# Half swap of a rotary embedding on ScalarE, its sine part and sum, four product steps and the lists of steps of a three-layer block changed

## The chip, the cores and the metric

One core of one Trainium2 chip. The metric is the device time of one launch in microseconds (us), the median of several runs. A core has TensorE (PE, matmuls; PEld is its weight load), VectorE (DVE), ScalarE (ACT), GpSimd (POOL) and SyncE (SP, which issues the DMAs here). Every engine works through its own list of instructions in order and meets the others only at semaphores.

## The reference, cut to what matters

The input x is 8 sequences ("batches") of 512 tokens with 128 features. Three layers follow one another:

```python
# 1. delta net, 8 heads x 16, two decays j per head
q, k = elu(x@Wq.T)+1, elu(x@Wk.T)+1 ; v = x@Wv.T
S = S*beta_eff + gate * outer(k, v)        # a scan over the tokens
z = z*beta_eff + gate * k
y = sum_j( (q.S)/(q.z + eps) * softmax(mix)_j )
x1 = layernorm(x + y@Wout.T + bout) * ln_g + ln_b
...
# 2. causal attention, 16 heads x 8, rotary positions
q = q*cos + rotate_half(q)*sin ; k = k*cos + rotate_half(k)*sin
out = softmax(mask(q@k.T * scale)) @ v ; out = out@proj_w.T + proj_b
...
# 3. feed-forward layer with the signs of a weight, behind norms
```

Everything is float32 in the reference. The kernel takes q and k of the attention apart into three bf16 parts each, so that bf16 matmuls give the scores to float32 precision.

## The kernel before, in words

**Stages.** The work of each batch b (0 to 7) is cut into stages: `norm` (statistics of x), `scan` (the delta net, in C = 4 chunks c of 128 tokens, each of two halves), `mid` (output projection, norms, the sign layer, then the projections and the rotation for attention), `maxima` (row maxima of the scores, for a stable softmax), `attn` (scores again, exponentials, products with the values) and `end` (projection and last norm). Each stage is a Python generator on each engine, and every `yield` is one step.

**Order.** The order of the steps on each engine is a string written out by hand or by a planner (`PE_ORDER`, `ACT_ORDER`, `DVE_ORDER`, `POOL_ORDER`, `SP_ORDER`): each letter (n, s, m, x, a, e) names the stage whose next step is issued. So stages of neighbouring batches are interleaved: while the maxima of batch b run, the scan and mid of batch b+1 run between them. Within a stage the order of the steps is fixed.

**Scan.** POOL writes `xe` for a chunk (L624); PE turns it into exponents (L977, L979); ACT takes their exponentials, `dec`, in two halves (L738); DVE multiplies them into `am` (L1504) and makes the decayed keys `kd` (`keys`, L1514); PE forms the state update from `kd` (L1008); DVE adds it to the state (`advance`, L1529 and L1533); POOL spreads the state over the heads (`spread_state`, L636); PE adds its part (L1044). At the end of a chunk (`finish`) DVE takes a reciprocal (L1540), multiplies it by the mix weights (L1544), scales (`ytmp`, L1547) and adds the two decays into `ytok` (L1554). ACT writes decay weights into `qp` and `bend` (L777, L778) and DVE multiplies `qp` by q (L1494). The first two batches (`EARLY` = 2) use more PSUM banks.

**Mid.** DVE adds the residual (`hres`, L1583), takes statistics (`norm_stats`, L1301 to L1317), and POOL takes the power -1/2 of four variances per partition (`rsqrt`, L593). Meanwhile DVE scales the residual by ln_g (`hg`, L1591). Then x1 (L1598), x2 (L1610) and the projections of q and k (PE L1123, sides 0 and 1, one PSUM bank `BK_MID`). For each side DVE makes the cosine part (`rope1`) in one instruction over 128 partitions and the sine part (`qkf`) in two over 64 partitions each, which read the other half's rows of PSUM; both are L1629. L1634 adds them. ACT (L836, L840) and DVE or POOL (L1638, L1652; L661, L665) split the sum into three bf16 parts, and SP writes these to DRAM (L532) and reads them back as stacked rows `qs` and `ks` (L543, L546).

**Maxima and attention.** For each half of the heads (22 groups) PE writes a bank of scores (L1167, L1169), and DVE reduces it to row maxima `mrow` (L1679); for batches 0 to 6 all groups share one PSUM bank, so a group's matmuls wait for the reduce of the group before. PE computes the scores again (L1196, L1199), ACT takes the exponentials (L873), PE multiplies by the values (L1215).

Of the kernel before, what the change touches and what calls it, by code (L numbers as in the profile page):

```python
# [10 lines left out]
ALU = mybir.AluOpType  # L11
# [4 lines left out]
P = 128  # L16
# [74 lines left out]
MID_STEPS = 28  # L91
# [6 lines left out]
    "sxssssssmssssssssssssssssssmsssssssssssssmssmsmsmsssssmmsssssssssssssmsssmsmssmsssssssssssssssssxsxmxxsx"  # L98
    "mxsxxsxxsxssxxsxsxsssxssxxssxsxsmssxxssmxssxssxasaxasaxassxaxssxsmxaamxssxasxsxmaxaaaxsaxmxsxsxamxsaxama"
    "asxaaaxaaasasxaassaxmaxaaxsxasaxsxaaaaxmaxsaaaasxaaxaasasaxsxaaxaassxaasxaaaxmaaxssexmxsxexssxmssxexexsm"  # L100
    "xeasxesaxsasxsaxsxsxsaxaaaxsaaxsxaxsaxasxaaxasaxmaaxmxasxaxaasaaxaxasxaaaaaxasxaamaaxasxaasxaxasxmxasxas"
    "axaasxasxaasxaasxasasxsxaaxaamxaaxsexmssxsxsexsmxasaxsxeaxssxssxexssxsaxsxeaxsexssxaaxamsaxasxaxasaxsaax"
    "asaxmsaamaaaxasasaamaaxsxaaaxamasxaasxaaxaaxsaxaasxsxaaxasxsxaaaxmsxamasxasaxamaaxsaxasxaaxasxssexsxssxm"
    "exssxeasxexsssaxaessxesxsxaaxssxsxaaaxasaxsxaaxssxaaaxaamaxasaxaxaamaaxsaxasxaaaxaaaxasxaaxaasxaaxmaasxs"
    "axaaxaxmxssaxasxsaxasxaaxasaxaaxamasxaaxsemsxsxesxsmxsaesxaassxeaxmxesxsxexssxsxsaxaaxssaxasaxsxaaxssxsa"
    "axasaaaxsaaxssaxaamsxamxaaxasxaaaxaaaxsaxsaxaxaamxasxaaaaxaxasxaaxasaxmxaaxasasxasaxaxaasxsaasxmexsmxess"
    "xsaaxmxessxsexsmaexssxexxasxsxxssxsaxsaasaxsasaxsxaaxssxsaaaxasaasaxassxaaaxmaaxmxaaxaaaaaxaaxaxaxamxaam"
    "xaaxaaxaaaxaaxaaxaaxmaaxmxaaxaaxaaxemxexmxexexxaaxeaxaxexaxxaxaxaxaaxaxaaxaxaaxaaxaaxaxaaaaxaaxaxaxxaaaa"
    "axxxaaaxxaaxxaxaaxxaxaaaaxaxaxxaaaaxaxaxaaaxaaxxexxxeaaxxaexaaxexxxaxaxaaxxaaxxaxaexxaxaaaaeaxaaaaaaaaaa"
# [3 lines left out]
    "nsssssxssssssssssssssssssssssnsmsmmsmsssssssssmssssssssssmmssssmmmsmssssnssssssmsssssssssssssssmssssxsaa"  # L113
    "aaassmmnasamaaasmmamamssssaaassaaaassaxssaassssasaaasamaaaaaaasaaaassaaaamaaaamsssssmxeeassasmaamaaamasa"
    "naaaamsaaaaaaxassasasaaaasaassaasmassassaasssaasaaasaaamsasaaamxssssasmaessaaseamaamamsaanaasamaaasaxaas"
    "sasamassasaaaasassasaasaasssamasamasaaaaaasamsaaxssssseammseaassmaaaanaasaaaaaaamsaaaxaasaasaaaassaaasaa"
    "ssmasassasssssaaasaaaamaaasamxssamseanssaessamamsamaassaaaaaasaaxamasaaaaaaasasaassaamasasaassaasasasasa"
    "asaassaasmaxmssaamsemmsemsasssasaaasasaaaaaasaxaaamaaaaaaaaaaamaaaaaaaaamaamaaaaaaxmeaameaaammaaaaaaaaaa"
    "aaaaxaaaaaaaaaaaaaaaaaaaaaaaaaaxaaaaeaaaaaaaeaaaaaxaaaaaaaaaaaaaaaaaaaaaaaaaaaaaaaee"
)  # L120
DVE_ORDER = (
    "nnnnxsssssssssnmnsmnnsssssssmsssmsmsmssssssssssssmsssssssssssssmmmmmmsssssmmsmmmsmmnsssssmsmnmsssssnssnm"
    "msmmmmsmmmmmsssssssssssssssssssssxxssxsxsxsmxmxmsxmsxxxxsxsxsmmsxsmxsxxmxsssxssmxssmxsxxsxxmnmxssxssxssx"
    "mnmmxnmnxssxssxsssxmsxmxsmsxsmxmxmsxxmxsxssxxssmsxssxmxmxmxmxsmsmmxxxxxsnxsxnnmnssxmsmxxmxmmxssmmxxxsxss"
    "sxssaxaxmxmxmxaxxxaxmmxssaxssxsaxsassxmasaxmxsxaxsxssxssxxsxxsxssxsxxxmsxmxxxxxmsmsmmxmxmssmxsxssxnmxsnx"
    "nsxnmxxmxmxmsxssmxsxmsxxxsxsxxaxxxaxxmssxsmsxssxaxaxssxmxmssxssxssxaxsaxasaxamxamxssxssxsxsxmxsssxsxxxxs"
    "sxsmmmmmmmmssxsxssxnxmnnsxmsmnxxmxmxmmxmxsxsxsxsxmxmsmxmxmxmxsxsxxxxxssasxasxssaxamxssxaxassxssssxsaxsaa"
    "xxaxxssxssxssxxsxsssxxxxxxxxmmsmssxmxmmxmxmxmssxsxssxmnxnsxmsxxxxmxmxmsmnxmsxsxsxsxxxxaxnxammxssaxamxmss"
    "xmsxasxssxaxamxasasxmxaxssxssxssxxxsxxsssxsssxsxxxxsxsssxxmxmxmsxmssmxxmxmxssxsxsxsxmxmsxmsmxxmxmxmmxmsx"
    "sxxxxxssaxsamxmxamxamxssmxmaxssxaxssxssxaxsasaxmxaxsssxsssxxxxssxssssxxsxxsxssxssxxmxmxmmmmxxmxmxmxmmxmx"  # L130
    "mxmxmmxxxxxmxmxmxxxaxmxamaxaxmxmxaxaxmxaaaxmxaxmxmxxxxxxxxxxxxxxxxxxxxxxxxxxxxxxxxxxxxxxxxxxxaaxxaaxxxxx"
    "axxxxxxxxxxxxxxxxxaaaaaaaaaaaaaaa"
)
POOL_ORDER = (
    "nnssssnssnsssssmnmsssmsssssssnnsxssmnssssmssnsmnsxsmmmmmnsnssmsmssssmasmsmnmsxmnmssmnsssssmssnammmssxmnm"
    "ssmssmssssmmnsamsnsxmnmssnmsnsmssasmsmmssxsmmssmssmmmssasmxsssnsnmmmaxaa"
)
SP_ORDER = "nxnmmmmmmmmnxmmmmmmmxnmxmmammmmmxnmxammmmmmmxnmxmmmmmammxnmxmammmmmmxmxmmmmmammxmmxmmmmmmxmxaxaa"
# [16 lines left out]
def hybrid_block(nc, x, weights, vectors, consts, consts_bf, ones, scratch, out):  # L155
    with ExitStack() as ctx:
# [180 lines left out]
        hres_ready = sem("hres_ready")  # L337
        var_mid = sem("var_mid")
# [5 lines left out]
        proj_qk = sem("proj_qk")  # L344
# [1451 lines left out]
```

## Time and profile before

| | |
|---|---|
| median of 3 runs | 686.31 us (685.63 to 686.48) |
| span of the profiled execution | 679.2 us; its own time outside the span isn't in the profile, and the median lies 7.1 us above the span |
| busy share of the span | PE 86%, PEld 50%, DVE 80%, ACT 61%, POOL 32% |
| mean granted clock of TensorE | 0.955 |

A busy share is an average over the whole span. The stage that matters is read from windows, and which engine ends last there from the waits.

### The profile page before, as it was taken

How to read it: one execution, taken by the hardware profiler on the slowest of the kernel's cores; microseconds unless marked ns; L12 is line 12 of the kernel's file. 1: busy time of each engine (PE TensorE's matmuls, PEld its weight loads, DVE VectorE, ACT ScalarE, POOL GpSimd, SP SyncE). 2: the span in 40 equal slices, each digit the busy share in tenths (PEclk: the TensorE clock that was granted, in tenths of full speed). 3: DMA queues.
4: the chain of work that ended last, by engine and by line, in shares of the span. 5: the costliest groups of instructions: out<-in, count | busy, mean ns of one | idle time of the engine just before them, and what ended most of it. 6: DMA issues, size and time to landing. Idle time of an engine off the chain costs nothing.

```text
span 679.2 us, 16869 instructions
## 1 busy us (share of the span) xinstructions
PE 587.1 (86%) x6352; PEld 338.2 (50%) x6352; DVE 542.6 (80%) x1547; ACT 414.9 (61%) x884; POOL 216.5 (32%) x255
## 2 busy tenths in 40 slices
PE   3686876888989899999999999999999999788995
PEld 2344534445545555555644655464646554434543
DVE  5677774889877988889899879898799877966842
ACT  2754652545777467864795767775695566346583
POOL 5261631353243251434432521535033531000000
PEclk9689787599989999999999999999999999979999
DMA  3710027000460035201540054005400433054000
GB/s 118 120 22 1 17 74 111 7 18 2 92 112 6 10 82 90 47 3 34 104 88 1 27 111 77 15 10 112 76 15 27 83 57 46 18 103 74 18 19 15
DMA packets 24914, 35.07 MB, mean 52 GB/s; under 512 B 4857, under 2 KB 22265, under 8 KB 22521
## 3 DMA queue, kind: packets, MB, share of 16 engines
q1 hardware_dynamic: 24834, 34.01, 25.4%
q8 instruction: 50, 0.82, 0.5%
q14 instruction: 30, 0.25, 0.1%
HBM read 22.85 MB, written 8.39 MB: 46 GB/s over the span
## 4 chain that ended last, share of the span: by engine, by line
PE 34%; DVE 27%; issue 14%; DMA 9%; POOL 7%; ACT 6%; SPq 2%; POOLq 0%; DVEq 0%; ACTq 0%
DVE mrow L1679 8%; DMA qs<-consts_bf 7%; PE ps L1215 5%; PE ps L1167 4%; PE ps L912 4%; DVE qkf L1629 3%; PE ps L1199 2%; PE ps L1196 2%; PE ps L1169 2%; PE ps L992 2%; SPq L543 2%; DVE am L1504 2%; POOL xe L624 2%; PE ps L907 2%; DMA scratch<-parts 1%
## 5 line engine op out<-in xcount | busy, mean ns | idle before, releaser
L1679 DVE TENSOR_REDUCE mrow<-ps 128x1 f32<-128x384 f32 (+3 forms) x352 | 220.5, 634 | 66.6 <-PE ps L1169 64.2
L873 ACT ACTIVATE pT<-ps 128x512 f32<-128x512 f32 (+1 forms) x330 | 173.9, 556 | 94.9 <-PE ps L1199 84.4
L1167 PE MATMUL ps<-ks,qs 72*128 72x128 bf16 (+2 forms) x384 | 101.2, 284 | 25.1 <-DVE mrow L1679 23.3
L1169 PE MATMUL ps<-ks,qs 123*128 123x128 bf16 x512 | 92.2, 226 | 6.2 <-DMA qs<-consts_bf 4.6
L1199 PE MATMUL ps<-qs,ks 75*128 75x256 bf16 (+2 forms) x384 | 93.8, 276 | 0.0
L1196 PE MATMUL ps<-qs,ks 123*128 123x128 bf16 x512 | 88.7, 223 | 5.2 <-ACT pT L873 2.4
L1215 PE MATMUL ps<-pT,va 128*32 128x512 f32 (+1 forms) x960 | 89.4, 449 | 1.8 <-DVE xk L1736 0.7
L636 POOL TENSOR_TENSOR spread<-state,cst 128x144 f32<-128x144 f32 x112 | 47.3, 444 | 121.1 <-DVE state L1533 85.1
L1167 PEld LDWEIGHTS ps<-ks,qs 72*128 72x128 bf16 x384 | 36.8, 98 | 96.7 <-DVE mrow L1679 85.8
L1196 PEld LDWEIGHTS ps<-qs,ks 123*128 123x128 bf16 x512 | 45.4, 98 | 60.9 <-ACT pT L873 26.3
L593 POOL TENSOR_TENSOR mid_rstd<-mid_ve,half 128x4 f32<-128x4 f32 x24 | 28.7, 1194 | 138.5 <-DVE mid_ve L1317 138.5
L624 POOL TENSOR_TENSOR xe<-lpart,hot 96x1024 bf16<-96x1024 bf16 x32 | 60.4, 1896 | 35.5 <-DVE lpart L1490 35.5
L738 ACT ACTIVATE dec<-ps 128x512 f32<-128x512 f32 x64 | 38.1, 598 | 41.8 <-PE ps L979 41.7
L1169 PEld LDWEIGHTS ps<-ks,qs 123*128 123x128 bf16 x512 | 46.9, 100 | 19.9 <-issue 9.7
L728 ACT ACTIVATE qM<-qT,cst 128x256 f32<-128x256 f32 x128 | 53.5, 499 | 0.0
L1504 DVE TENSOR_TENSOR am<-dec,ps 128x1024 f32<-128x1024 f32 x32 | 38.8, 1213 | 6.8 <-PE ps L992 6.6
L1199 PEld LDWEIGHTS ps<-qs,ks 75*128 75x128 bf16 x384 | 38.0, 99 | 4.9 <-issue 1.7
L992 PE MATMUL ps<-qM,kT 128*64 128x512 f32 x128 | 37.0, 642 | 0.0
L1024 PE MATMUL ps<-am,vg 128*32 128x128 f32 x1024 | 36.1, 283 | 0.0
L797 ACT ACTIVATE yT<-ps,epsc 128x512 f32<-128x512 f32 x32 | 21.9, 683 | 18.2 <-PE ps L1024 17.9
L1215 PEld LDWEIGHTS ps<-pT,va 128*32 128x32 f32 x960 | 19.6, 108 | 23.5 <-issue 10.1
L593 POOL TENSOR_TENSOR attn_rstd<-attn_ve,half 128x4 f32<-128x4 f32 x8 | 8.2, 1025 | 68.3 <-DVE attn_ve L1317 68.3
(209 smaller groups left out, 1091.5 us busy)
## 6 DMA issues: line engine op xcount, KB each, us to landing
ks<-scratch SPq DMA_DIRECT2D x48, 192.0 KB
scratch<-parts SPq DMA_DIRECT2D x48, 128.0 KB, 1.8
qs<-scratch SPq DMA_DIRECT2D x32, 128.0 KB
qs<-scratch SPq DMA_DIRECT2D x16, 192.0 KB
x<-x SPq DMA_DIRECT2D x8, 256.0 KB, 3.3
qs<-scratch SPq DMA_DIRECT2D x32, 64.0 KB
out<-xk SPq DMA_DIRECT2D x8, 256.0 KB, 2.3
qs<-pT SPq DMA_DIRECT2D x3, 384.0 KB, 9.2
```

What stands on the lines that cost most here:

```text
L624: pool.tensor_tensor(xe[rows, c % 2, :, :], lpart[rows, c, :].unsqueeze(1).broadcast_to([PARTS * QUAD, HJ, LB]), hot[rows, :].unsqueeze(2) ...
L636: ins = pool.tensor_tensor(spread[:, n % SLOTS, j, :, :].rearrange("p (g i) e -> p g i e", i=2), state[:, n % PAIRS, j, :].rearrange("p (i ...
L728: ins = act.activation(qM[:, h, :], qT[:, cp * 2 * P:(cp + 1) * 2 * P], ACT.Copy, scale=headmask[:, h:h + 1])
L873: act.activation(probs(b, g, kt)[:, c0:c0 + m, :], ps[:, score_bank(b, n), 0:m * width].rearrange("p (m n) -> p m n", n=width), ACT.Exp, s ...
L992: mm = pe.matmul(ps[LB * q:LB * q + LB, bank_g(b, c), :], kT[:, at:at + LB], qM[:, :, at - (c // 2) * 2 * P:at - (c // 2) * 2 * P + LB], s ...
L1167: pe.matmul(o[:, 0:qt * P], qs[0:K_MAX, f % RING, h, own_tile], ks[0:K_MAX, f % RING, h, 0:qt * P], start=True, stop=True, skip_group_chec ...
L1169: mm = pe.matmul(o[:, own_tile], qs[0:K_DIAG, f % RING, h, own_tile], ks[0:K_DIAG, f % RING, h, own_tile], start=True, stop=True, skip_gro ...
L1196: mm = pe.matmul(o[:, 0:P], ks[0:K_DIAG, place, h, own_tile], qs[0:K_DIAG, place, h, own_tile], start=True, stop=True, skip_group_check=True)
L1199: mm = pe.matmul(o[:, P:width], ks[0:K_ALL, place, h, own_tile], qs[0:K_ALL, place, h, (kt + 1) * P:T], start=True, stop=True, skip_group_ ...
L1215: mm = pe.matmul(ps[q:q + QUAD, values_bank(b, g), kt * P:T], va_columns(b, kt, g, i), probs(b, g, kt)[:, i, :], start=(kt == 0 and g % 2 ...
L1504: dve.tensor_tensor(am[:, c % 2, :, :, :], dec[:, c % 2, :, :].rearrange("p (h j) t -> p h j t", j=J), gq.unsqueeze(2).broadcast_to([P, H, ...
L1679: dve.tensor_reduce(mrow[:, qt, h0:h0 + m], ps[:, max_banks(b)[n % len(max_banks(b))], 0:m * width].rearrange("p (m k) -> p m k", k=width) ...
```

## The change

1. **Rotation.** For each side ACT copies the two halves of the projection from PSUM, swapped, with the bias, into `qkf` (two instructions of 64x512). DVE makes only the cosine part (one instruction), and waits for ACT's copies first. POOL multiplies `qkf` by the sine table in place, and then adds the cosine part. PE's next projection waits for DVE's cosine part. The sine table's minus sign moves to the other half, as rows are now multiplied after the swap.
2. **Scaled residual.** `hg` is computed by POOL, ahead of its first `rsqrt` of the batch.
3. **Products of the scan**, for batches 2 to 7 (`products_aside`): `qp` times q, the decayed keys `kd`, and the sum `ytok` are computed by POOL. In POOL's list a chunk is now: `xe` of the next chunk, `kd` of the next chunk, `ytok` of the chunk before, then the state spreads. DVE's `ytmp` waits for the `ytok` before it.
4. **All five order strings are new.** On PE each stage of each batch starts and ends at nearly the same count of maxima steps as before.

```diff
+        def products_aside(b):
+            return b >= EARLY
...
+                def weighted(cp):
+                    pool.wait_ge(pdec_ready, b * 2 + cp + 1)
+                    pool.wait_ge(qk_ready, b * 2 + 1)
+                    pool.tensor_tensor(qp[:, cp, :, :, :], qp[:, cp, :, :, :],
...
+                def keys(c):
+                    pool.wait_ge(dec_ready, b * 8 + 2 * c + 2)
+                    pool.wait_ge(ktok_ready, b + 1)
+                    pool.wait_ge(su_ps, b * 7 if c < 2 else b * 7 + 2 * c - 2)
...
+                def joined(c):
+                    pool.wait_ge(y_free, b * 4 + c + 1)
+                    if c == 0:
+                        pool.wait_ge(turned, b * 3 - 2)
...
                 yield
                 decay_rows(0)
+                if products_aside(b):
+                    for cp in range(2):
+                        yield
+                        weighted(cp)
+                    yield
+                    keys(0)
                 for c in range(C):
                     if c + 1 < C:
                         yield
                         decay_rows(c + 1)
+                        if products_aside(b):
+                            yield
+                            keys(c + 1)
                     if c > 0:
+                        if products_aside(b):
+                            yield
+                            joined(c - 1)
                         yield
                         spread_state(2 * c)
...
             def mid(b):
                 for n in range(3):
+                    if n == 0:
+                        yield
+                        pool.wait_ge(hres_ready, b + 1)
+                        if b > 0:
+                            pool.wait_ge(xk_ready, b)
+                            pool.wait_ge(x2n_ready, b)
+                        pool.tensor_tensor(hg[:, :, :], hres[:, :, :], row_vector(vec, V_LNG),
+                                           ALU.mult).then_inc(hg_ready, 1)
                     yield
                     rsqrt(var_mid, b * 3 + n + 1, mn, rstd_mid)
+                for side in range(2):
+                    yield
...
+                    pool.wait_ge(halves, b * 2 + side + 1)
+                    pool.tensor_tensor(qkf[:, side, :], qkf[:, side, :], sinT[:, :], ALU.mult).then_inc(sined, 1)
+                    yield
+                    pool.wait_ge(sined, b * 2 + side + 1)
+                    pool.wait_ge(roped, b * 2 + side + 1)
+                    pool.tensor_tensor(qkf[:, side, :], rope1[:, side, :], qkf[:, side, :], ALU.add).then_inc(qk_full, 1)
...
+                for side in range(2):
+                    yield
+                    act.wait_ge(proj_qk, b * 2 + side + 1)
...
+                    for to, rows in ((lower, upper), (upper, lower)):
+                        ins = act.activation(qkf[to, side, :], ps[rows, BK_MID, :], ACT.Identity,
+                                             bias=bcol[rows, side:side + 1])
+                    ins.then_inc(halves, 1)
...
+                    if b * 4 + c > 0:
+                        dve.wait_ge(y_ready, b * 4 + c)
                     dve.tensor_tensor(ytmp[:, :, :], yv[:, :, 0:DH], over_features(rec[:, :], DH),
                                       ALU.mult).then_inc(y_free, 1)
+                    if products_aside(b):
+                        return
...
+                    dve.wait_ge(halves, b * 2 + side + 1)
+                    dve.scalar_tensor_tensor(rope1[:, side, :], ps[:, BK_MID, :], bcol[:, side:side + 1],
+                                             cosT[:, :], ALU.add, ALU.mult).then_inc(roped, 1)
```

## Rows read from the trace of the kernel before

**Rows 1.** Busy time of each engine in stretches; clock, DMA share and GB/s last
```profile
core 0: us, PE busy (x) PEld busy (x) DVE busy (x) ACT busy (x) POOL busy (x), PEclk, DMA share, GB/s
...
113.00:550.00 437.00, 402.88 (x4527) 233.36 (x4526) 381.06 (x1071) 288.16 (x620) 161.64 (x183) 0.97 0.26 51
0.00:113.00 113.00, 77.32 (x801) 47.10 (x802) 75.85 (x262) 55.47 (x122) 46.92 (x65) 0.86 0.31 65
550.00:679.00 129.00, 106.93 (x1026) 57.70 (x1026) 85.74 (x214) 71.29 (x142) 7.91 (x8) 0.97 0.22 42
```

**Rows 2.** Who PE waited for, 113 to 550 us: us, times, longest us
```profile
PE ps L1167 <- DVE mrow L1679: 15.2, 31, 1.4
...
PE ps L944 <- DVE kT L1478: 2.4, 5, 0.8
...
PE ps L1123 <- DVE qkf L1629: 1.0, 2, 0.8
```

**Rows 3.** Groups of instructions by line, whole span: busy us, mean ns, idle before
```profile
L1629 DVE SCALAR_TENSOR_TENSOR qkf<-ps,bcol,sinT 64x512 f32<-64x512 f32 x32 | 24.0, 750 | 0.8
...
L1514 DVE TENSOR_TENSOR kd<-ktok,dec 128x256 f32<-128x256 f32 x32 | 13.5, 423 | 0.5 <-issue 0.3 <-ACT dec L738 0.2
...
L1634 DVE TENSOR_TENSOR qkf<-rope,qkf 128x512 f32<-128x512 f32 x16 | 11.6, 726 | 0.0
L1494 DVE TENSOR_TENSOR qp<-qp,qT 128x512 f32<-128x512 f32 x16 | 11.3, 716 | 3.1 <-ACT bend L778 3.1
...
L1554 DVE TENSOR_TENSOR ytok<-ytmp 128x128 f32<-128x128 f32 x32 | 9.5, 297 | 0.5
...
L1591 DVE TENSOR_TENSOR x<-hres,vec 128x512 f32<-128x512 f32 x8 | 5.5, 685 | 0.0
```

**Rows 4.** The same view: what POOL and ACT take for like shapes
```profile
L636 POOL TENSOR_TENSOR spread<-state,cst 128x144 f32<-128x144 f32 x112 | 47.3, 444 | 121.1 <-DVE state L1533 85.1 <-DVE state L1529 32.1 <-PE ps L1044 3.7
...
L803 ACT ACTIVATE midT<-ps 128x512 f32<-128x512 f32 x24 | 14.3, 597 | 2.7 <-PE ps L907 2.6
L661 POOL TENSOR_TENSOR rope<-qkf,parts 128x512 f32<-128x512 f32 x12 | 14.1, 1176 | 27.7 <-ACT parts L836 27.7
...
L607 POOL TENSOR_TENSOR xb<-x,vec 128x512 f32<-128x512 f32 x8 | 10.2, 1275 | 16.0 <-DVE x L1598 13.7 <-DMA w<-weights 2.2
```

**Rows 5.** DVE and POOL instructions in order of time: start us, us
```profile
82.83 0.52 DVE L1544 TENSOR_TENSOR rec<-rec,mixw 128x16 f32<-128x16 f32 x1
...
81.43 1.89 POOL L624 TENSOR_TENSOR xe<-lpart,hot 96x1024 bf16<-96x1024 bf16 x1
...
367.36 1.49 DVE L1634 TENSOR_TENSOR qkf<-rope,qkf 128x512 f32<-128x512 f32 x1
...
367.14 1.16 POOL L661 TENSOR_TENSOR rope<-qkf,parts 128x512 f32<-128x512 f32 x1 [1.30 <-ACT parts L836]
```

**Rows 6.** One batch's scan in order of time, POOL, ACT and PE
```profile
441.94 1.90 POOL L624 TENSOR_TENSOR xe<-lpart,hot 96x1024 bf16<-96x1024 bf16 x1
...
442.03 0.57 ACT L738 ACTIVATE dec<-ps 128x512 f32<-128x512 f32 x1
...
451.96 0.60 ACT L738 ACTIVATE dec<-ps 128x512 f32<-128x512 f32 x1
...
444.55 0.70 PE L1044 MATMUL ps<-spread,qp 128*64 128x144 f32 x4
...
457.92 0.71 PE L1044 MATMUL ps<-spread,qp 128*64 128x144 f32 x8
```

**Rows 7.** Batch 0's rotation on DVE and PE, and the loads behind it
```profile
85.76 0.75 DVE L1629 SCALAR_TENSOR_TENSOR rope<-ps,bcol,cosT 128x512 f32<-128x512 f32 x1 [0.95 <-PE ps L1123]
...
92.09 0.69 DVE L1634 TENSOR_TENSOR qkf<-rope,qkf 128x512 f32<-128x512 f32 x1
...
88.11 1.56 PE ps L1123 x2
...
101.28 11.00 DMA qs<-consts_bf
```

More of the change, by code:

```diff
@@ L830, in mid @@
                 turn_out(3)
+                lower, upper = slice(0, P // 2), slice(P // 2, P)
+                for side in range(2):
+                    yield
+                    act.wait_ge(proj_qk, b * 2 + side + 1)
+                    if b == 0:
+                        act.wait_ge(bias_sb, 1)
+                    else:
+                        act.wait_ge(part2, b * 2)
+                    for to, rows in ((lower, upper), (upper, lower)):
+                        ins = act.activation(qkf[to, side, :], ps[rows, BK_MID, :], ACT.Identity,
+                                             bias=bcol[rows, side:side + 1])
+                    ins.then_inc(halves, 1)
                 for side in range(2):
@@ L1396, in setup_mid @@
                             ins = dve.tensor_scalar(o[:, s, :, :], table[:, c, :].unsqueeze(1).broadcast_to([P, HA, DA // 2]),
-                                                    -1.0 if n == 1 and s == 1 else 1.0, None, ALU.mult)
+                                                    -1.0 if n == 1 and s == 0 else 1.0, None, ALU.mult)
                     ins.then_inc(cos_tok, 1)
@@ L1490, in scan @@
                 dve.tensor_tensor(lpart[third, :, :], lres[third, :, :], lpart[third, :, :], ALU.subtract).then_inc(lpart2, 1)
-                for cp in range(2):
+                for cp in range(0 if products_aside(b) else 2):
                     yield
@@ L1555, in finish @@
                                       yj[:, :, 1, :], ALU.add).then_inc(y_ready, 1)
[L1557 to L1558 removed]
+                if not products_aside(b):
+                    yield
+                    keys(0)
                 yield
@@ L1617, in mid @@
                 yield from norm_stats(s, x2, mn, var_mid)
-                lower, upper = slice(0, P // 2), slice(P // 2, P)
                 for side in range(2):
-                    for n, (dst, table, moves) in enumerate(((rope1, cosT, ((slice(0, P), slice(0, P)),)),
-                                                             (qkf, sinT, ((lower, upper), (upper, lower))))):
-                        yield
-                        if b == 0:
-                            dve.wait_ge(bias_sb, 1)
-                        else:
-                            dve.wait_ge(part2, b * 2)
-                        dve.wait_ge(proj_qk, b * 2 + side + 1)
-                        for to, rows in moves:
-                            ins = dve.scalar_tensor_tensor(dst[to, side, :], ps[rows, BK_MID, :], bcol[rows, side:side + 1],
-                                                           table[rows, :], ALU.add, ALU.mult)
-                        ins.then_inc(roped, 1)
-                    yield
-                    dve.wait_ge(roped, b * 4 + 2 * side + 2)
-                    dve.tensor_tensor(qkf[:, side, :], rope1[:, side, :], qkf[:, side, :], ALU.add).then_inc(qk_full, 1)
+                    yield
+                    if b == 0:
+                        dve.wait_ge(bias_sb, 1)
+                    else:
+                        dve.wait_ge(part2, b * 2)
+                    dve.wait_ge(halves, b * 2 + side + 1)
+                    dve.scalar_tensor_tensor(rope1[:, side, :], ps[:, BK_MID, :], bcol[:, side:side + 1],
+                                             cosT[:, :], ALU.add, ALU.mult).then_inc(roped, 1)
                 for side in range(0 if residues_aside(b) else 2):
```

105 lines of the change are left out of this document (59 added, 46 removed).

## The prediction

> **What bounds the kernel now.** The busy shares of the whole span (PE 86%, DVE 80%) mix three regimes, so I read the windows first. Before 113 us there are no maxima yet: the chain of batch 0 ends in a load of 11.00 us that nothing shortens [rows 7]. PE is busy for 77.32 of 113 us there, idle for 35.7. From 113 to 550 us PE is busy for 402.88 of 437 us (92%), DVE for 381.06 (87%), POOL for 161.64 (37%) [rows 1]. Behind 550 us PE is idle for 22.1 of 129 us. In all PE idles for 92 us, and no relief of another engine can take more than that away.
>
> Then I read who PE waited for in the long stretch [rows 2]. The largest wait names DVE's row maxima (15.2 us in 31 times): each group of maxima matmuls needs the bank that the reduce before it empties, and the reduce stands in DVE's list among other work. The next two that name DVE are 2.4 us (the scan's k) and 1.0 us (the rotation). That is 18.6 us of the 34.1 us of idle PE. The rest is scattered in many small waits. So PE is the engine that sets the pace, and DVE, nearly as full, makes it wait a little. A faster DVE can give back only what stands in these waits.
>
> **What leaves DVE.** The two sine instructions of each side: 4 a batch, 0.750 us each, 3.00 us. The sums: 2 x 0.726 = 1.45 us. The scaled residual: 0.685 us. That is 5.1 us in every batch. In batches 2 to 7 also `qp`, 2 x 0.716 = 1.43 us, `kd`, 4 x 0.423 = 1.69 us, and `ytok`, 4 x 0.297 = 1.19 us: 9.45 us a batch in all [rows 3]. Over the launch: 6 x 9.45 + 2 x 5.1 = 67 us. Some 57 us of it lie between 113 and 550 us, where the mids of batches 1 to 6 and nearly all the scans of 2 to 7 are. DVE's 381 us there become 324, or 74% of the stretch.
>
> **What POOL takes.** No row shows these very instructions on POOL; the nearest are the residue L661 (128x512, both inputs dense, 1.176 us), L607 (128x512, one input a repeated row, 1.275 us) and L636 (128x144, 0.444 us) [rows 4]. By these a batch's sine products and sums cost 4 x 1.18 = 4.7 us, `hg` 1.28 and `qp` 2 x 1.28 = 2.6. For `kd` (256 elements) a line between L636 and L607 gives 0.444 + 112/368 x 0.83 = 0.70 us; its bounds are those two rows, 0.44 and 1.28. `ytok` (128 elements) lies at L636's end, 0.4 us, between 0 and 0.44. Four of each: 2.8 and 1.6. Sum 13.0 us for a late batch, 6.0 for the first two, 90 us in all. In the long stretch POOL goes from 162 us to about 240, 55%. It isn't full, but its list is in order.
>
> **What ACT takes.** Four instructions of 64x512 a batch. The nearest row is the 128x512 copy from PSUM, 0.597 us [rows 4]: 2.4 us a batch, 19 us in all, on an engine busy for 288 of 437 us. I count it at nothing while it hides behind PE's other work; as all of it delays the rotation alone, its price is in the next term.
>
> **The rotation's own chain.** In batch 0 it runs from 85.76 us, when side 0's projection has been written, to 92.78 us (92.09 + 0.69), 7.0 us, with PE's second projection of 1.56 us in the middle [rows 7]. Now: two copies 2 x 0.60, cosine 0.75, projection 1.56, two copies 1.2, sine product 1.18, sum 1.18 (the cosine of side 1 hides behind the sine product). That is 7.1 us, and about 0.1 us for each of some five handovers, against four before: 7.0 becomes about 7.5. The chain is no shorter; it only takes less of DVE. In the middle, where the stacked rows are loaded well ahead of use, the 0.5 us costs nothing; if that cover is gone it is 0.5 us a batch.
>
> **The sum.** Middle: what of the 18.6 us goes. The lower bound is 0 (the wait is the bank's round trip, matmul and reduce, which isn't shortened), the upper all 18.6. A reduce stands behind others' work less often when DVE is 74% full instead of 87%, but a part of each wait is the round trip itself. I take 45%, 8.4 us. Head: of the 5.1 us taken from DVE in mid 0, between nothing and all is felt by the chain, and the rotation costs 0.5: from +0.5 to -4.6, I take -1.5. Tail: batch 7's rotation precedes its loads, and there DVE's list is also crowded; 4.45 us leave it and 0.5 come: from +0.5 to -4.0, I take -1.5. Waits for POOL that are new (PE for `kd`, `qp`, `ytok`; DVE's `ytmp` for the `ytok` before it, with reduces queued behind; x1 for `hg`): +1.0, where nothing is the lower end and the upper is the rival below. The new lists keep each stage at the same count of maxima steps, so I give the reordering nothing of its own. Sum: -8.4 - 1.5 - 1.5 + 1.0 = -10.4 us. The profiled span of 679.2 us would become 668.8; with the 7.1 us between span and median, the median 686.3 becomes 676.
>
> **Contention.** Two rows show DVE and POOL getting in each other's way [rows 5]. A DVE product of 16 elements, L1544, takes 0.52 us and ends at 83.35 us, just behind POOL's `xe` (81.43 + 1.89 = 83.32). L1634 takes 1.49 us instead of its mean of 0.726, started inside POOL's L661 that ended at 368.30. Both have two inputs in SBUF, and both waited until POOL was done. The Trainium skill says the same (SBUF — State Buffer, "Who interferes with whom"): a DVE instruction with two SBUF inputs contends with a GpSimd instruction that reads SBUF, and whichever starts first holds the other off entirely. By that rule, the trace agrees, a fuller POOL is dearer for DVE than its own sum shows. But the five groups that leave DVE are mostly of this kind (all but the sine parts), 13 instructions a late batch. That is why I take no net cost in the sum.
>
> **Rivals.**
>
> *POOL's list is late (slower).* The new POOL list puts `kd` of the next chunk ahead of the spread of this chunk's state. In one late batch the second half of `dec` for chunk 1 ends at 442.60 [rows 6]; `kd` would end at 443.30, two spreads (0.89) at 444.19, and PE's L1044 that needs them started at 444.55: 0.36 us to spare, less the handovers. For chunk 2 POOL would stand from the end of `xe` (443.84) to the end of `dec` (452.56), 8.7 us, with spreads, `rsqrt` and the residues behind it unless the list puts them ahead; L1044 of the next chunk came at 457.92. If a POOL instruction of 1.2 us comes into each of these margins, that is 0.8 us in 18 chunks (6 batches, 3 each): +14.4, and 676 + 14.4 = 690. It decides from 10.4 / 18 = 0.58 us of delay a chunk. For it: these thin margins, and `hg`, sine and sum in the same list. Against it: POOL idled 121 us ahead of the spreads, waiting for DVE [rows 4], so it mostly has room to be later. Chance 0.17.
>
> *PE is simply full (no change).* The waits for the reduce are round trips or change their name, and head and tail stay: 686. For it: PE at 92%. Against it: 31 waits of up to 1.4 us aren't all round trips. Chance 0.13.
>
> *Contention gives half of it back.* About 40 short DVE instructions a batch with two SBUF inputs remain (statistics, gates, mix weights). POOL's share rises by 0.18; a meeting costs about 0.5 us, half a POOL instruction: 40 x 6 x 0.18 x 0.5 = 22 us of DVE, less what the 13 moved ones met, 13 x 6 x 0.37 x 0.5 = 14: 7 or 8 us net, on the path at worst: 683. Chance 0.10. The rule of the skill named above is this one's.
>
> *DVE was the bound all along.* Then most of the 34.1 us of idle PE in the middle goes with the 57 us: some 26 us, 660. For it: PE's weight loads fill 233 of 437 us only [rows 1], and matmul spans overlap, so 92% overstates how full PE is. Against it: in the list of waits PE's idle time is small whatever its name. Chance 0.10. The Trainium skill (Perfetto Trace Analysis, "Identifying the Most-Contended Engine") says that matmul busy time misjudges how near PE is to its limit and that the share of weight loads tells more; by it this rival would be likelier, and no row here decides it.
>
> **The numbers.** My forecast, 676, has 0.50; its own range is 670 to 682. A difference under 0.2% (1.4 us) can't be told from none here. Faster: 0.50 + 0.10 + 0.10 = 0.70. Same: 0.13. Slower: 0.17. The range for 8 in 10 cuts off the deeper half of the last rival and the upper half of the first: 664 to 690.
>
> **What would show it.** In the profile after: the three stretches [rows 1] added up and changed by the sums above give DVE busy for 543 - 67 = 476 us, POOL 216 + 90 = 306, ACT 415 + 19 = 434; PE's waits for `mrow` in the middle at about half of 15.2 us; a second projection that waits for ACT's copies and the cosine part; POOL products near the prices above. Wrong would be: PE waits that name POOL's `kd`, `spread` or `ytok` for more than a few us; `kd` on POOL above 1 us; a start of the first maxima later than 113 us; reduces that wait behind `ytmp`.

## The result and the profile after

| | median us | ratio to before, 95% interval |
|---|---|---|
| before | 685.97 | |
| changed kernel | 700.09 | 1.0226 [1.016, 1.0292] |

The changed kernel is 2.3% slower; 676 was forecast, in a range that ended at 690. Its profiled execution took 703.15 us with a span of 701.4. The two profiled spans lie 22.2 us apart and the medians 14.1, since the profile of the kernel before is of one of its quicker executions; stretches of the two traces can be compared, but their differences add up to more than the median's loss. The engines' busy time, from the page of the changed kernel:

```profile
span 701.4 us, 16916 instructions
PE 590.3 (84%) x6322; PEld 342.1 (49%) x6352; DVE 533.6 (76%) x1431; ACT 436.2 (62%) x916; POOL 301.4 (43%) x355
```

ACT came out as forecast (434 forecast), POOL nearly (306). DVE did not: 476 us were forecast, and it fell from 543 to 534 only. The same three stretches as in [rows 1]:

```profile
0.00:113.00 113.00, 72.88 (x741) 42.57 (x751) 79.31 (x241) 56.17 (x121) 52.87 (x68) 0.89 0.26 57
113.00:550.00 437.00, 387.89 (x4315) 229.51 (x4327) 357.68 (x951) 295.24 (x629) 223.68 (x257) 0.96 0.26 49
550.00:702.00 152.00, 129.57 (x1285) 70.05 (x1278) 96.64 (x241) 84.79 (x167) 24.88 (x31) 0.93 0.26 49
```

PE gets through fewer matmuls in the long stretch (4,315 against 4,527) and idles for 49 us of it, not 34. The first reduce of the row maxima starts at 124.12 us (113.04 before), the last at 670.89 (649.19), and 30.5 us follow (30.0). So 11 us are lost ahead of the first maxima, 10.6 between first and last, and nothing behind them. Who PE waited for from 113 to 550 us in the changed kernel, to be held against [rows 2]:

```profile
PE ps L1245 <- DVE mrow L1750: 20.4, 36, 4.8
PE ps L1253 <- DVE mparts L1767: 6.9, 7, 2.8
PE ps L1247 <- DVE mrow L1750: 2.6, 3, 1.4
```

The wait that was to be halved has grown from 15.2 us to 20.4, with a longest of 4.8 us where it was 1.4. No row of this view names POOL's `kd`, `spread` or `ytok`. What the moved work costs on POOL, from the groups of the changed kernel:

```profile
L719 POOL TENSOR_TENSOR qkf<-qkf,sinT 128x512 f32<-128x512 f32 x16 | 20.4, 1274 | 25.9 <-ACT qkf L906 25.9
L723 POOL TENSOR_TENSOR qkf<-rope,qkf 128x512 f32<-128x512 f32 x16 | 20.3, 1268 | 2.8 <-DVE rope L1704 2.3
L662 POOL TENSOR_TENSOR kd<-ktok,dec 128x256 f32<-128x256 f32 x24 | 15.4, 641 | 45.9 <-ACT dec L804 45.9
L653 POOL TENSOR_TENSOR qp<-qp,qT 128x512 f32<-128x512 f32 x12 | 15.1, 1267 | 8.4 <-ACT bend L844 8.4
...
L672 POOL TENSOR_TENSOR ytok<-ytmp 128x128 f32<-128x128 f32 x24 | 11.0, 456 | 32.1 <-DVE ytmp L1627 32.1
...
L710 POOL TENSOR_TENSOR x<-hres,vec 128x512 f32<-128x512 f32 x8 | 10.2, 1271 | 57.5 <-DVE hres L1667 57.5
```

They sum to 92.4 us, against 90 in the forecast. So the sum of the prices was right, and the place to look is DVE. Its groups with shapes kept apart show instructions that the change didn't touch and that are longer than they were:

```profile
L1677 DVE SCALAR_TENSOR_TENSOR x<-x,mid_rstd,xb 128x128 f32<-128x128 f32 x32 | 12.5, 451 | 2.5 <-POOL mid_rstd L601 2.4
L1383 DVE TENSOR_TENSOR mid_mv<-mid_stats 128x4 f32<-128x4 f32 x24 | 9.0, 373 | 0.1
L1383 DVE TENSOR_TENSOR scan_mv<-scan_stats 128x4 f32<-128x4 f32 x8 | 6.8, 852 | 0.0
L1389 DVE SCALAR_TENSOR_TENSOR scan_mv<-scan_mv 128x4 f32<-128x4 f32 x8 | 4.1, 518 | 0.0
L1757 DVE TENSOR_SCALAR mparts<-mrow 128x32 bf16<-128x32 f32 x16 | 5.2, 325 | 0.4
L1474 DVE TENSOR_SCALAR x<-cst 128x64 f32<-128x64 f32 x16 | 5.0, 411 | 0.0
```

In the same order their means were 346, 173, 154, 184, 176 and 238 ns before. The statistics work on four numbers a partition; nothing in them can take 852 ns. Over all groups whose count didn't change, DVE's instructions last 45 us longer in sum. The trace in order of time shows why. DVE of the changed kernel around 320 us, where the longest of these instructions stands:

```profile
319.14 0.55 DVE L1750 TENSOR_REDUCE mrow<-ps 128x1 f32<-128x384 f32 x1
319.61 5.40 DVE L1383 TENSOR_TENSOR scan_mv<-scan_stats 128x4 f32<-128x4 f32 x1
324.92 0.15 DVE L1384 SCALAR_TENSOR_TENSOR scan_mv<-scan_stats 128x4 f32<-128x4 f32 x1
325.00 0.15 DVE L1386 SCALAR_TENSOR_TENSOR scan_mean<-scan_stats 128x4 f32<-128x4 f32 x1
```

POOL in the same stretch:

```profile
319.04 1.27 POOL L719 TENSOR_TENSOR qkf<-qkf,sinT 128x512 f32<-128x512 f32 x1
320.27 1.27 POOL L621 TENSOR_TENSOR xnb<-xn,vec 128x512 f32<-128x512 f32 x1
321.50 1.26 POOL L723 TENSOR_TENSOR qkf<-rope,qkf 128x512 f32<-128x512 f32 x1
322.72 2.26 POOL L727 TENSOR_TENSOR rope<-qkf,parts 128x512 f32<-128x512 f32 x2
```

A subtraction of 0.15 us lasts 5.40 us. It ends at 325.01, just behind POOL's fifth instruction in a row (322.72 + 2.26 = 324.98). This is the mechanism of [rows 5], some seven times as long as the longer delay there, beside a run of POOL work with no gap in it. Most delays are shorter and end with the first POOL instruction that they meet, even when the next one follows at once. DVE near 389 us:

```profile
388.82 1.29 DVE L1764 CAST mparts<-mres 128x32 bf16<-128x32 f32 x1
```

POOL beside it:

```profile
388.81 1.26 POOL L723 TENSOR_TENSOR qkf<-rope,qkf 128x512 f32<-128x512 f32 x1
390.03 1.26 POOL L621 TENSOR_TENSOR xnb<-xn,vec 128x512 f32<-128x512 f32 x1
```

The cast ends at 390.11, between the two. For a measure of all this I take each DVE form at its quiet length (its 20th percentile) and add up what instructions exceed it by, where that is over 0.06 us, and note the POOL instruction that ended last beside each. I call the sum the **excess**. It is 5.0 us in 13 instructions before, 46.3 us in 67 in the changed kernel, all of it beside POOL's work. Of the 67, 61 wait for one POOL instruction only (27 of these with the next one following at once), and six wait through two or more. `xe` carries 14.3 us, and 35 of the 46 us stand beside instructions that were on POOL before the change.

### The profile page after: what moved, and what is told of

Same layout as the page of the kernel before. It is cut to its first block, busy times and chain, and to the rows that moved or that the text cites. A ratio compares the mean times of both kernels' runs of the same rounds, so it can differ in the third digit from the quotient of the medians.

```text
span 701.4 us, 16916 instructions
## 1 busy us (share of the span) xinstructions
PE 590.3 (84%) x6322; PEld 342.1 (49%) x6352; DVE 533.6 (76%) x1431; ACT 436.2 (62%) x916; POOL 301.4 (43%) x355
## 4 chain that ended last, share of the span: by engine, by line
PE 42%; issue 23%; DVE 23%; POOL 7%; ACT 5%; DMA 0%; POOLq 0%; DVEq 0%; ACTq 0%
PE ps L1293 5%; DVE mrow L1750 5%; PE ps L990 5%; PE ps L1245 5%; PE ps L1070 3%; PE ps L1102 3%; PE ps L1274 2%; PE ps L1277 2%; PE ps L1247 2%; PE ps L985 2%; PE ps L1122 2%; POOL xe L632 2%; DVE am L1582 2%; PE ps L1111 2%; PE ps L1201 1%
## 5 line engine op out<-in xcount | busy, mean ns | idle before, releaser
L1293 PE MATMUL ps<-pT,va 128*32 128x512 f32 (+1 forms) x960 | 90.9, 455 | 3.9 <-ACT pT L951 3.5
L601 POOL TENSOR_TENSOR mid_rstd<-mid_ve,half 128x4 f32<-128x4 f32 x24 | 25.0, 1040 | 74.8 <-DVE mid_ve L1395 74.8
L1070 PE MATMUL ps<-qM,kT 128*64 128x512 f32 x128 | 39.7, 663 | 0.0
L662 POOL TENSOR_TENSOR kd<-ktok,dec 128x256 f32<-128x256 f32 x24 | 15.4, 641 | 45.9 <-ACT dec L804 45.9
L710 POOL TENSOR_TENSOR x<-hres,vec 128x512 f32<-128x512 f32 x8 | 10.2, 1271 | 57.5 <-DVE hres L1667 57.5
```

The lines of the kernel that those rows point to most:

```text
L1070: mm = pe.matmul(ps[LB * q:LB * q + LB, bank_g(b, c), :], kT[:, at:at + LB], qM[:, :, at - (c // 2) * 2 * P:at - (c // 2) * 2 * P + LB], s ...
L1293: mm = pe.matmul(ps[q:q + QUAD, values_bank(b, g), kt * P:T], va_columns(b, kt, g, i), probs(b, g, kt)[:, i, :], start=(kt == 0 and g % 2 ...
```

## Experiments

Each ratio is to the kernel before, timed beside the run on the same chip. What "lists" means is the hand-written order of each engine's steps.

### Reads or mere occupation of POOL: e1, e2

The kernel before, with 11 more POOL instructions a batch, one at each reciprocal root but the scan's, and one at each spread, that nobody waits for. Nothing is left out. The second writes as long, but reads nothing.

```
...
+ pool.tensor_tensor(idle, both, both, ALU.add)        # e1: 128x512, 88 times
+ pool.memset(idle, 1.0); pool.memset(idle, 1.0)       # e2: 128x512 each, 88 times two
```

> The kernel before, unchanged, with 88 more instructions on POOL that nobody waits for: behind each state spread and each power, one product-sized addition of 512 elements that reads a constant in SBUF and writes a spare tile, about 1.27 us each, 112 us in all (the change adds 85). Theory contention (DVE instructions with SBUF inputs wait until POOL's instruction is over): DVE's busy time grows by 30 us or more in the same instructions, and the time rises to 695 to 710. Theory late list (POOL's own products come late, the rest is as before): the time rises as much as with the next kernel, and DVE's instructions keep their durations. Theory full PE (nothing but PE counts): 686.

> The same places in POOL's list, with two memsets of 512 elements each instead of the addition, which only write the spare tile, about 1.1 to 1.2 us together. Theory contention on reads: DVE's two-input instructions keep their durations of the kernel before, and the time is below that of the kernel with additions by 8 us or more. Theory late list: the same time as the kernel with additions, within 3 us.

Measured: e1 720.66 us, 1.0551 [1.0465, 1.0638]; e2 704.18, 1.0303 [1.0219, 1.0386]. The group of the additions in e1:

```profile
L608 POOL TENSOR_TENSOR idle<-cst 128x512 f32<-128x512 f32 x88 | 92.9, 1056 | 0.0
```

The group of the memsets in e2:

```profile
L608 POOL MEMSET idle<- 128x512 f32 x176 | 93.1, 529 | 5.1
```

The same 93 us on the same list differ by 16.5 us of time, and in little but whether they read. e1 is 10 us above the range of the contention theory, and in e2 DVE's two-input instructions did not keep their lengths. The excess is 39.0 us with reads and 23.6 with writes, of which the memsets stand beside 4.0 and the rest is POOL's own older work, shifted. e2's own 20 us were not taken apart: the shifted excess is in them, and POOL's list may be later, since these lists were made for a POOL without this work.

### Lists alone, moves alone: e3, e4, e7, e8

e3 has every instruction where it was before, but the new lists; the steps that are in no new list follow their neighbour. e4 has all the moves in the lists of before; e7 only the rotation, e8 only the products. Nothing is left out.

```
  ROT, HG, PQ, PK, PY = 0, 0, 0, 0, 0    # e3, new lists
  ROT, HG, PQ, PK, PY = 1, 1, 1, 1, 1    # e4, lists of before
  ROT, HG, PQ, PK, PY = 1, 0, 0, 0, 0    # e7, lists of before
  ROT, HG, PQ, PK, PY = 0, 1, 1, 1, 1    # e8, lists of before
```

> The work of every engine as in the kernel before, but in the new order lists: steps that had moved to POOL or ACT are left out there and stand on DVE again, right behind or ahead of the step that they belong to. Theory lists (the new order itself costs): 692 to 700, first row maxima later than 118 us. Theory contention: 684 to 689.

> All the moves of the change (rotation, scaled residual, the three products of the scan), in the order lists of the kernel before: PE's and SP's unchanged, DVE's with the moved steps taken out, POOL's and ACT's with them put in at the times at which DVE had them in the trace of before. Theory contention: 695 to 706, DVE's same instructions 30 us or more longer. Theory lists: 676 to 686.

> Only the rotation moved (half swap on ACT, sine part and sum on POOL), in the order lists of the kernel before with the moved steps put in at the times at which DVE had them. It takes 36 us off DVE. Theory contention: few more collisions, 684 to 695. Theory fragile lists (a step that comes in a list ahead of its inputs holds up all behind it): 700 or more, with POOL standing at its sine products for ACT's copies.

> Only the three products of the scan moved, in the order lists of the kernel before with the moved steps put in at the times at which DVE had them. It takes 26 us off DVE. Theory contention: 684 to 695. Theory fragile lists: 700 or more, POOL standing at the decayed keys for the decays with the spreads behind.

| run | median us | ratio, 95% interval | DVE busy us | excess us |
|---|---|---|---|---|
| e3 new lists | 740.92 | 1.083 [1.076, 1.09] | 576.5 | 30.3 |
| e4 moves | 733.72 | 1.0716 [1.0632, 1.08] | 500.3 | 15.7 |
| e7 rotation | 695.25 | 1.0174 [1.0098, 1.025] | 515.3 | 9.1 |
| e8 products | 715.93 | 1.0438 [1.0324, 1.0551] | 534.7 | 13.8 |

The placement and the lists don't come apart: the new lists without the moves (e3) and the moves without the new lists (e4) are both 5 to 6% slower than the two together, and both are slower than either theory had them. The rotation and the products each cost something by themselves; e8's time is in the range of "fragile lists", e7's at the edge of "contention". In e4 the excess is small, so contention is not most of what costs there; in part PE waits for POOL, as the first rival had it. From e4's waits, whole span:

```profile
PE ps L1246 <- DVE mrow L1778: 28.3, 52, 2.4
PE ps L1123 <- POOL spread L645: 17.1, 7, 5.9
```

So a late POOL list is a real danger for this placement. In the changed kernel, with its new lists, no row of PE's waits names the spread. What the changed kernel lost in time is not told by these four runs. Where its meetings come from is, in part: with the new lists and not one moved instruction (e3) POOL is as little busy as before (215.4 us, against 216.5), and the excess is 30.3 us where it was 5.0; with all the moves in the old lists (e4) POOL is busy for 300.7 us, and the excess is 15.7. In these two runs the order of the lists weighs more than how full POOL is.

### The reads taken out: e5, and its control e6

Every computing instruction of POOL is a memset of like length in its place, with the same waits and increments. What POOL computed is left out: x with its mask, the spreads, reciprocal roots, sums, products and residues.

```
- pool.tensor_tensor(dst, a, b, op).then_inc(sem, 1)
+ pool.memset(idle[:, 0:k], 1.0)                       # once or twice, to the same length
+ pool.memset(dst, 0.5).then_inc(sem, 1)
```

> The changed kernel with every addition, product and power of POOL replaced by memsets of about the same length in the same places with the same waits (it leaves out all that POOL computes, so its output has no meaning; constants flow on instead). POOL reads nothing from SBUF any more. Theory contention (DVE's instructions wait for POOL's reads, 46 us of DVE's time in the changed kernel): DVE's busy time falls by 35 us or more and the time to 675 to 687. Theory lists (the new order costs by itself): 696 to 704.

> The same replacement in the kernel before, as the control: there DVE loses only 5 us to POOL. Both theories: 680 to 690. A time far from that would say that the memsets are too short or too long, and by how much.

Measured: e5, the changed kernel, 668.55 us, 0.9764 [0.9666, 0.9861]; e6, the kernel before, 687.08, 1.0018 [0.9974, 1.0062]. From the page of e5:

```profile
PE 580.3 (87%) x6352; PEld 336.2 (50%) x6352; DVE 492.3 (74%) x1431; ACT 435.4 (65%) x916; POOL 313.2 (47%) x859
```

Its long stretch in the view of windows:

```profile
113.00:550.00 437.00, 404.97 (x4651) 238.75 (x4650) 351.65 (x1002) 310.10 (x661) 247.05 (x683) 0.98 0.28 53
```

Its largest PE wait there:

```profile
PE ps L1261 <- DVE mrow L1793: 10.8, 23, 1.0
```

POOL is as busy as in the changed kernel, its list and its waits are the same, and 31.5 us are gone, with 38.7 of the excess (46.3 to 7.6); the time is below the range of either theory. Of the 7.6 us that are left 5.2 stand on 18 `TENSOR_SCALAR` instructions; those with two tensor inputs have 1.2, where they had 35.9. POOL's reads cost the changed kernel 1.0226 - 0.9764 = 4.6% and the kernel before nothing that can be measured. The first rival falls with this run as the cause: the same POOL list, with the same waits and as full, gives 668. A lower clock of TensorE is not the cause either: an execution of the changed kernel with a granted clock of 0.956 took 697.0 us, and those of the kernel before at 0.955 in the runs of e5 and e6 took 680 to 689. Between the first and the last maxima the clock was 0.96 in the changed kernel and 0.97 before and in e5; what part of the loss goes through that was not taken apart.

### Which reads: e9, e10

As e5, but only some of POOL's instructions are memsets: in e9 the six groups that the change moved there, in e10 the older ones. What they compute is left out.

```
- pool.tensor_tensor(qkf, qkf, sinT, ALU.mult)         # e9: L719, L723, L662, L653, L672, L710
- pool.tensor_tensor(xe, lpart, hot, ALU.mult)         # e10: all the others
+ fill(...)
```

> The changed kernel, with only the products and sums that the change moved to GpSimd (sine part, sum, decay products, gated sum, scaled residual) as memsets of like length, their results left out; GpSimd's older instructions (x with mask, normalised x, state copies, column sums) still read. Theory 'the older reads now meet VectorE at bad moments': in the trace of the changed kernel the moved instructions stand beside 11 of 46 us of VectorE's excess, the older ones beside 35; with 31.5 us of time lost in all, 31.5 x 11/46 = 7.5 us come back: 692 to 693 us, excess about 35 us. Rival 'the added reads do it': the older reads cost the kernel before nothing (687 against 684 us), so with the new ones gone nearly all of it comes back: 668 to 674 us, excess under 12 us.

> The counterpart: the changed kernel with GpSimd's older reading instructions as memsets of like length, their results left out, and the moved products and sums real. Theory 'older reads at bad moments': 668.6 + 7.5 = 676 us, VectorE's excess about 11 us. Rival 'the added reads do it': 694 to 700 us, excess 35 us or more. If both kernels come out near 684, each kind has its half.

Measured: e9 687.23 us, 1.0005 [0.9973, 1.0037], excess 30.0; e10 675.80, 0.9827 [0.9787, 0.9867], excess 21.1. Against the changed kernel's 1.0226, taking the older reads out gives 4.0%, taking the new ones out 2.2%, and both (e5) 4.6%. e10's time is the one that the first theory expected, though its excess is 10 us above it; e9 lies between the theories (1.1%, and 3.8% or more). The two gains sum to more than both at once, which fits with delays such as that at 319.61, in a run of both kinds. So the older reads are worth between 2.4% (e9 against e5) and 4.0% of the 4.6%, by which kind is taken out first (e5's own interval is 1% to either side): by the medians the larger part of the loss is work that stood on POOL all along and cost nothing there (e6). By the excess of e3 and e4 its meetings with DVE's short instructions come mainly with the new lists; what they cost in time there was not separated.

### The held instructions: e11, and its control e12

The variance of each norm comes from one aggregating instruction a chunk, with one SBUF input, in place of a chain with two inputs. Nothing is left out.

```
- s.counted(dve.tensor_tensor(nb.mv[:, 0, :], m0, m1, ALU.subtract))
- s.counted(dve.scalar_tensor_tensor(nb.mv[:, 1, :], v0, D * LN_EPS, v1, ALU.add, ALU.add))
...
+ for c in range(C):
+     s.counted(dve.bn_aggr(nb.mv[:, c, :], nb.stats[:, c, :]))
+ dve.tensor_scalar(nb.ve[:, :], nb.mv[:, :, 1], LN_EPS, None, ALU.add).then_inc(done, 1)
```

> The changed kernel, with the variance of each norm formed from bn_aggr (four instructions of one SBUF input) and one tensor_scalar, in place of a chain of three to five VectorE instructions with two SBUF inputs each. Nothing is left out. Theory 'two SBUF inputs wait for GpSimd's reads': these chains carry 18 of the 46 us of excess; 31.5 x 18/46 = 12 us come back, less some 3 us for about 150 more short instructions: 688 to 694 us, and the aggregating instructions show no maximum near 1 us. Rival 'the delay is of any VectorE instruction, or moves to the next one': 699 to 706 us, and the new instructions are stretched as the old ones were.

> The kernel before with the same norms by bn_aggr; nothing is left out. Both theories: its chains hardly met GpSimd (5 us of excess in all), so what shows is only the price of about 150 more short instructions: 684 to 689 us. Were it under 681, the two-input chains cost the kernel before as well.

Measured: e11 688.42 us, 1.0006 [0.9978, 1.0034], excess 35.5; e12 686.69, 0.995 [0.9908, 0.9993]. Of the 2.3% lost, 2.2% come back (12 us between the medians), by changing which instructions DVE has while POOL does what it did. The same edit gives the kernel before 0.5%, so about 1.7% of it belong to the changed kernel alone. Groups of DVE in e11:

```profile
L1384 DVE BATCH_NORM_AGGREGATE mid_mv<-mid_stats 128x2 f32<-128x6 f32 x96 | 8.8, 154 | 0.1
L1384 DVE BATCH_NORM_AGGREGATE scan_mv<-scan_stats 128x2 f32<-128x6 f32 x32 | 2.9, 152 | 0.0
L1388 DVE TENSOR_SCALAR scan_mean<-scan_mv 128x4 f32<-128x4 f32 x8 | 4.2, 526 | 0.0
```

None of the 160 aggregating instructions is held (152 to 154 ns in the mean, the longest 183), though 56 of them began and ended within one reading POOL instruction. The `TENSOR_SCALAR` behind them is, with one SBUF input. And part of the delay moved on: POOL's same sum and residues, with the `kd` behind them, now hold another product with two inputs. DVE of e11 there:

```profile
315.04 3.89 DVE L1616 TENSOR_TENSOR rec<-rec,mixw 128x16 f32<-128x16 f32 x1
```

POOL of e11 in that stretch:

```profile
314.81 1.27 POOL L724 TENSOR_TENSOR qkf<-rope,qkf 128x512 f32<-128x512 f32 x1
316.04 2.27 POOL L728 TENSOR_TENSOR rope<-qkf,parts 128x512 f32<-128x512 f32 x2
318.26 0.64 POOL L663 TENSOR_TENSOR kd<-ktok,dec 128x256 f32<-128x256 f32 x1
```

### Shorter POOL instructions: e13 to e16

e13 cuts `xe` into two of 96x512. e14 does the same to every 128x512 instruction of POOL too. e15 joins e14 with e11; e16 is e15's edits in the kernel before. Nothing is left out.

```
- pool.tensor_tensor(xe[rows, c % 2, :, :], ..., ALU.mult).then_inc(xe_ready, 1)
+ for half_j in (slice(0, HJ // 2), slice(HJ // 2, HJ)):
+     ins = pool.tensor_tensor(xe[rows, c % 2, half_j, :], ..., ALU.mult)
+ ins.then_inc(xe_ready, 1)
```

> The changed kernel, with the 96x1024 product of x with the mask on GpSimd (32 of 1.9 us) issued as two of 96x512. Nothing is left out. Theory 'a delay lasts as long as the GpSimd instruction met': its 14.3 us of excess fall to about half, 7 us, worth 31.5 x 7/46 = 5 us: 694 to 696 us. Rival 'the total reading time decides': 700 us or a little more, since 32 more instructions are issued, and the excess beside them stays at 14 us.

> The changed kernel, with every 128x512 GpSimd product, sum and difference, and that of 96x1024, issued as two halves; nothing is left out. Theory 'a delay lasts as long as the instruction met': excess from 46 to 25 us or less, of 31.5 us lost some 14 come back: 684 to 689 us, if about 120 more GpSimd instructions cost nothing on its own list. Rival 'total reading time': 700 to 706 us, excess 46 us or more, now in more and shorter delays.

> The halves together with one-input statistics, in the changed kernel; nothing is left out. If both theories hold and add, 688 less 10 to 14 us: 674 to 679 us, faster than both kernels. If the length of an instruction does not matter: 688 to 692 us.

> The same two edits in the kernel before; nothing is left out. It has 5 us of excess, so neither theory gives it anything to win: 681 to 688 us. Were it as fast as the changed kernel with the same edits, the change itself would be worth nothing even without the meetings.

| run | median us | ratio, 95% interval | excess us (in) |
|---|---|---|---|
| e13 | 699.05 | 1.0224 [1.0151, 1.0296] | 46.2 (71) |
| e14 | 699.55 | 1.0192 [1.0131, 1.0254] | 42.2 (81) |
| e15 | 688.09 | 1.0045 [1.0007, 1.0084] | 33.1 (60) |
| e16 | 683.03 | 0.9943 [0.9902, 0.9983] | 7.7 (18) |

My theory fell here: halves give nothing. In e13 the excess beside `xe` is 14.4 us, where it was 14.3. DVE near 533 us in e13:

```profile
532.87 0.91 DVE L1788 TENSOR_SCALAR mparts<-mrow 128x32 bf16<-128x32 f32 x1
533.81 0.97 DVE L1791 SCALAR_TENSOR_TENSOR mres<-mrow,mparts 128x32 f32<-128x32 f32 x1
534.82 0.18 DVE L1795 CAST mparts<-mres 128x32 bf16<-128x32 f32 x1
```

POOL of e13 at that place, its two halves in one row:

```profile
532.70 2.04 POOL L634 TENSOR_TENSOR xe<-lpart,hot 96x512 bf16<-96x512 bf16 x2
```

The first half holds the first step of the chain, the second half the next: two delays of 0.73 and 0.78 us for one of 1.59 at this place of the changed kernel. POOL's halves have no gap between them, so for a chain of short steps they are one instruction, though each step by itself was let in between them. The 5.4 us delay of the changed kernel is in e13 too, at 5.54 us. What counts here is for how long POOL reads beside the chain, and not the length of one of its instructions.

The fastest kernels that compute the whole are e12 and e16, the kernel before with one-input statistics (in e16 with the halves too): 0.5 and 0.6% faster than before, the intervals just clear of 1. The change has no part in it: with the same edits (e15 against e16) it is 1% slower.

## Why the prediction was wrong

**The step that failed** is the one under *Contention*: "That is why I take no net cost in the sum." It measured 31.5 us of time (e5 against the changed kernel), and nothing in the kernel before (e6). Without it, the rest of the sum had the right sign: some 16 us gained in e5 (1 - 0.9764), 10.4 forecast. Engines thus meet at more than their semaphores: DVE and POOL also met at POOL's reads.

Three things in that step were off. It set the instructions that leave DVE (13 a late batch, met by POOL at the share of its busy time) against those that stay. But the kernel before hardly had meetings, 13 in all with 5.0 us; its lists kept DVE's short two-input steps and POOL's work apart (with the new lists alone e3 has 44 meetings with 30.3 us), and a share of busy time can't see that. Leaving DVE therefore saved almost nothing of this kind, and "I give the reordering nothing of its own" was wrong too. Second, the price of a meeting was taken as half a POOL instruction, 0.5 us. In the changed kernel it is 46.3 / 67 = 0.69 us in the mean, and 5.2 us in the one case where it lasted through five POOL instructions. Third, it counted new work on POOL only, while three quarters of the excess stand beside POOL's older work; e9 and e10 put 2.4 to 4.0% of the 4.6% lost on it.

**The rival "contention gives half of it back"** had the mechanism and an 0.10 chance, at 7 or 8 us. It was mis-sized by a factor of four. That the time rose at all had another 0.17, for a late POOL list, which is not what happened (e5). The rule that the contention rival rested on holds. The Trainium skill (SBUF — State Buffer, "Who interferes with whom") says that a DVE instruction with two SBUF inputs contends with GpSimd's reads and not with its writes: by e1 and e2, 16.5 us apart, and e5, the runs agree. The same section of the Trainium skill names `tensor_scalar` and casts as able to take the shared ports too, under conditions on their operands that I did not go through; the cast at 388.82, L1474, L1757 and e11's L1388 were held. What it says of the length, that the one that issues first has the ports for its whole instruction and the other is blocked, fits the 61 delays of 67 that waited for one instruction; it is less than the row at 319.61 shows, where the wait went through five in a row.

**Middle.** -8.4 us was forecast from three rows of PE's waits, 18.6 us together. In e5 they fell to 10.8 for `mrow`, 0.3 for `kT` and none for the rotation: 7.5 us less, near the forecast. Yet first to last maxima took 14.7 us less there. The windows from the first to the last maxima, before and in e5:

```profile
113.04:649.19 536.15, 487.50 (x5332) 279.23 (x5331) 457.36 (x1249) 341.94 (x727) 167.53 (x188) 0.97 0.26 51
116.32:637.81 521.49, 477.30 (x5322) 277.70 (x5322) 413.32 (x1139) 358.68 (x753) 255.48 (x704) 0.97 0.27 52
```

PE's idle time fell by 4.5 us only; the other 10.2 us are busy time of PE, for as good as the same matmuls at the same clock. So "a faster DVE can give back only what stands in these waits" does not hold; why the busy time shrank was not taken apart. In the changed kernel first to last maxima took 10.6 us more than before.

**Head.** -1.5 us was forecast (+0.5 to -4.6); it was +11 us, and +3.3 without reads (first maxima at 116.32 in e5). A start of the first maxima later than 113 us was one of the prediction's own signs of being wrong. The rotation's chain was sized right: from ACT's first copy at 90.23 us to the end of the second sum at 96.70 + 1.26, 7.7 us, against 7.5 in the forecast. ACT of the changed kernel, side 0:

```profile
90.23 1.38 ACT L906 ACTIVATE qkf<-ps,bcol 64x512 f32<-64x512 f32 x2 [0.26 <-PE ps L1201]
```

The second sum on POOL:

```profile
96.70 1.26 POOL L723 TENSOR_TENSOR qkf<-rope,qkf 128x512 f32<-128x512 f32 x1
```

It began late. Far ahead of it, DVE's first instruction of a group of eight (238 ns in the mean before) is held:

```profile
36.58 2.83 DVE L1474 TENSOR_SCALAR x<-cst 128x64 f32<-128x64 f32 x1
```

POOL beside it:

```profile
36.21 1.89 POOL L632 TENSOR_TENSOR xe<-lpart,hot 96x1024 bf16<-96x1024 bf16 x1
38.06 1.27 POOL L621 TENSOR_TENSOR xnb<-xn,vec 128x512 f32<-128x512 f32 x1
```

It ends at 39.41, just behind POOL's 39.33. DVE's state update just ahead of it was 2.7 us later than in the kernel before already (36.25, against 33.55); the decayed keys behind it are 4.7 later (40.58, against 35.92, and 35.72 in e5, without POOL's reads). Batch 0's scan stays 3.5 to 6.7 us late from there to the rotation (first cosine part at 91.71, where it was 85.76), and the loads of the maxima's operands are issued from 105.46 us on, where it was 98.21. The remaining 3.8 us between these loads and the first maxima were not taken apart.

**Tail.** -1.5 was forecast; 30.0 us became 30.5.

**DVE's busy time.** 67 us of instructions left it, and busy time fell by 9. Of the difference, 45 us are longer instructions. Some of the rest is that busy time counts overlap once: the two rows at 324.92 and 325.00 start 0.08 us apart and last 0.15 each, so an instruction that leaves takes less with it than its length. In e5, with little excess, busy time fell by 50 us for the same 67.

**New waits for POOL.** +1.0 was forecast; no PE wait in the middle names the moved work, and the sum of POOL's prices held to 3%. One by one they were further off: the sine product and the sum took 1.27 us each for 1.18, `kd` 0.64 for 0.70, and `ytok` 0.456 for 0.4, just above its upper bound of 0.44.

**From span to median.** 7.1 us were added to the span. In the changed kernel only 1.8 us lie outside it (703.15 less 701.4); the rest was that the profile before is of a quicker execution than the median. It stands on both sides of the comparison, so the forecast gain doesn't hang on it.

**PE full, DVE the bound all along.** e5 speaks against both: with contention gone the changed kernel gains 2.4%, more than the first allows and some 60% of what the second gave (16 us of 26).

## What to carry to other kernels

Before work is moved to GpSimd, price two things beside its own duration: which short VectorE instructions with SBUF inputs will stand beside any GpSimd instruction in the new order, and how long GpSimd reads without a gap there. Look at the lengths of untouched VectorE instructions after such a change: a form whose mean grew from 154 to 852 ns tells it in one row. Cutting GpSimd's instructions in two gave nothing here; one-input forms in VectorE's short chains gave 12 us. A memset stand-in on GpSimd tells in one run, with a second as control, what its reads cost.

## What the runs showed of the hardware

- A VectorE subtraction of 0.15 us was held for 5.40 us, through five GpSimd instructions that followed each other without a gap. That is the exception: of 67 delays 61 waited for one GpSimd instruction only, 27 of them with the next one following at once.
- A `TENSOR_SCALAR` with one SBUF input of 128x64 fp32 was held for 2.83 us by two GpSimd instructions; 160 aggregating instructions with one input were not held (longest 183 ns), 56 of them within a reading GpSimd instruction.
- 93 us of GpSimd memsets held VectorE for 4 us, 93 us of additions at the same places for 16.6 us beside themselves. With every GpSimd instruction a memset, 7.6 us of delays were left, 5.2 of them on `TENSOR_SCALAR`.
